# GpSimd's scatters of the second region wait, quad by quad, for TensorE's sums of the first

## The reference

```python
h = jnp.maximum(_layernorm(x, axis=-1), 0.0)
xw = feature @ weight
msgs = edge_weight[:, None] * xw[edge_col]            # one message of 128 floats per edge
agg = jax.ops.segment_sum(msgs, edge_row, num_segments=feature.shape[0])
new_feature = agg + bias                              # then batch norm, relu, two residuals
```

## Time and profile before

| | us |
|---|---|
| median of 3 runs | 5428.9 |
| lowest and highest | 5419.73, 5434.21 |
| span of the profiled execution | 5477.2 |
| TensorE busy (matmul) in it | 3042.5 |
| GpSimd busy in it | 3230.7 |

### The profile page before, as it was taken

One profiled execution on the slowest core, in us unless ns is written; L12 is line 12 of the kernel. 1 busy time (PEld: TensorE's weight loads), 2 busy tenths in 40 slices (PEclk: granted clock), 3 DMA queues, 4 the chain that ended last, 5 costly groups with the idle time before them and its releaser, 6 DMA issues.

```text
span 5477.2 us, 57778 instructions
## 1 busy us (share of the span) xinstructions
PE 3042.5 (56%) x16167; PEld 2620.6 (48%) x16167; DVE 2092.3 (38%) x5291; ACT 1457.9 (27%) x3880; POOL 3230.7 (59%) x3309
## 2 busy tenths in 40 slices
PE   6634444431595343333333787887785566666666
PEld 6534333321592232223223666766674455555555
DVE  8723222220362000000002444444445566666666
ACT  3211111100003232323333333333332233333332
POOL 2466666667203666666664666666663566666663
PEclk7666666665796555555555656555656777877778
DMA  3633333334463111111112333333332444444443
GB/s 103 185 106 114 115 112 111 108 128 130 160 232 118 45 45 47 44 47 45 47 45 71 94 90 93 90 94 93 91 94 77 121 133 133 133 134 132 132 134 85
DMA packets 262094, 563.24 MB, mean 103 GB/s; under 512 B 70904, under 2 KB 83065, under 8 KB 260860
## 3 DMA queue, kind: packets, MB, share of 16 engines
q0 software_dynamic: 119856, 280.99, 18.8%
q1 hardware_dynamic: 131858, 265.37, 14.6%
q10 hardware_dynamic: 10090, 13.23, 1.0%
HBM read 410.82 MB, written 150.10 MB: 102 GB/s over the span
## 4 chain that ended last, share of the span: by engine, by line
another core or an unknown queue 35%; PE 20%; issue 17%; DVE 15%; ACT 7%; DVEq 3%; POOL 1%; DMA 0%; ACTq 0%; POOLq 0%
ACT arena L897 4%; PE banks L1192 3%; PE banks L1179 3%; PE banks L1022 3%; PE banks L1002 2%; DVEq L1259 2%; PE banks L1009 2%; DVE work L1380 2%; ACT arena L904 2%; PE banks L1162 2%; PE banks L967 2%; DVE acc L1368 1%; DVE work L1867 1%; DVE work L1864 1%
## 5 line engine op out<-in xcount | busy, mean ns | idle before, releaser
L707 POOL DMA_INDIRECT work<-rel_table,idx_b x808 | 773.3, 957 | 682.9 <-DMA rel_table<-work 300.9
L723 POOL DMA_INDIRECT work<-kv_table,idx_a x808 | 776.3, 961 | 472.3 <-issue 217.1
L723 POOL DMA_INDIRECT work<-gat_table,idx_a x808 | 777.4, 962 | 469.9 <-issue 258.7
L692 POOL DMA_INDIRECT msgs<-work,idx_a x808 | 805.8, 997 | 394.4 <-issue 238.3
L1240 PE MATMUL banks<-work,arena 128*128 128x128 f32 x1616 | 387.4, 364 | 733.3 <-issue 661.2
L1022 PE MATMUL banks<-work,arena 128*128 128x136 f32 x3232 | 697.4, 375 | 66.6 <-issue 60.4
L790 ACT ACTIVATE arena<-iota,dst_local 128x128 f32<-128x128 f32 x1616 | 511.5, 388 | 733.8 <-remote 445.6
L1240 PEld LDWEIGHTS banks<-work,arena 128*128 128x128 f32 x1616 | 323.3, 266 | 800.8 <-issue 799.6
L1022 PEld LDWEIGHTS banks<-work,arena 128*128 128x128 f32 x3232 | 633.9, 277 | 102.6 <-issue 78.8
L1368 DVE TENSOR_TENSOR acc<-acc,banks 128x544 f32 x404 | 287.6, 712 | 921.2 <-remote 766.2
L1009 PE MATMUL banks<-nil 128*128 128x272 bf16 x1616 | 436.6, 363 | 36.6 <-issue 34.8
(11 more groups left out here) (320 smaller groups left out, 4701.2 us busy)
## 6 DMA issues: line engine op xcount, KB each, us to landing
work<-msgs SPq DMA_DIRECT2D x105, 516.0 KB
attr<-turned_all SPq DMA_DIRECT2D x204, 256.0 KB
turned_all<-work SPq DMA_DIRECT2D x202, 256.0 KB
w_rel<-turned_all SPq DMA_DIRECT2D x200, 256.0 KB
msgs<-work,idx_a POOLq DMA_INDIRECT x808
work<-rel_table,idx_b POOLq DMA_INDIRECT x808
work<-gat_table,idx_a POOLq DMA_INDIRECT x808
work<-kv_table,idx_a POOLq DMA_INDIRECT x808
```

What stands on the lines that cost most here:

```text
L692: nc.gpsimd.indirect_dma_start(msgs_all, bass.IndirectOffsetOnAxis(ap=idx_a[:, t:t + 1], axis=0), msg_ring[:, t % SPAN, :], None).then_inc ...
L707: nc.gpsimd.indirect_dma_start(row_ring[:, t % SPAN, :], None, rel_table, bass.IndirectOffsetOnAxis(ap=idx_b[:, t:t + 1], axis=0)).then_in ...
L723: nc.gpsimd.indirect_dma_start(ring[:, t % SPAN, :], None, table, bass.IndirectOffsetOnAxis(ap=idx_a[:, t:t + 1], axis=0)).then_inc(quad_i ...
```

## The change

Before each quad of region B, GpSimd now also waits until TensorE has summed a share of region A's halves. Quad `q` needs `82 * (q - 167) // 39` halves: none up to quad 167, then 2, 4, 6, 8, 10, 12, 14, 16, 18, 21 and so on, 71 for the last, quad 201. 34 quads have such a wait. Nothing is removed and no instruction changes its place on any engine.

```diff
+SUM_LAG = 4
...
+        def halves_due(q):
+
+            return HALVES_A * max(q - NQ_A - SUM_LAG, 0) // NQ_B
+
...
                 else:
                     late_wait(pool, q)
+                    if halves_due(q):
+                        pool.wait_ge(agg, at_agg["0b"] + HALF * halves_due(q))
                 for t in range(QUAD * q, QUAD * (q + 1)):
                     nc.gpsimd.indirect_dma_start(
```

## The result

| | before | changed |
|---|---|---|
| median of the timed runs, us | 5431.56 (4 runs, 5419.73 to 5440.97) | 5330.66 (4 runs, 5327.1 to 5334.71) |
| profiled execution, span, us | 5477.2 | 5332.9 |
| from the first scatter of region B to the last sum, us | 399.0 | 291.7 |
| of that, the scatters, us | 198.1 | 238.0 |
| from the last sum to the end, us | 3857.3 | 3824.2 |

What follows compares the result with a forecast made beforehand. Bound: scatters, then sums, in effect one after the other, as GpSimd's unbroken stream holds TensorE back. 11.3 cycles of 22.3 us, 252 us, then 61 us of sums: 60 us less, 5428.9 - 60 = 5369 us; range 5290 to 5560.

Steps and rivals of the forecast that it cites:

- holdback: Sums beside region B's scatters: TensorE's work held back and seen late, a half of 1.79 us taking 44.6.
- GpSimd's unbroken stream: Claimed cause: GpSimd's indirect DMAs without a break hold back what TensorE sends; a pause of GpSimd's lets it out.
- The first wait at 1246.5: Quad 168, which needs two halves, comes at 1246.5 us; GpSimd stops there.
- I take 7 us: Length of each GpSimd pause in region B, between 4.6 us (second layer) and 23.7 us (after the last scatter).
- After a pause the burst lasts 7 us: TensorE after each GpSimd pause: 3.9 halves in 7 us, as from 1231, plus some 2.6 done and not yet seen.
- GpSimd scatters three quads, 15.3 us: Scatters between two pauses in region B: 6.5 halves allow three quads, 15.3 us; with the pause, 22.3 us a cycle.
- the rival of nearly full overlap: First pause ends TensorE's delay, later stops keep it away: sums end at 1485, 134 us less, 5295 us; chance 0.12.
- After the scatters: Sums left once region B's scatters end: 34 halves, 61 us at full rate.
- A half beside GpSimd at 2.5 us: Sums beside scatters: loads, scatters and reloads share the DMA engines, so a half may take 2.5 us.
- Only SP waits for `msgs_done`: End of region B's scatters: only SP waits for `msgs_done`, at half 82, and its delay is covered.
- Long pauses: Rival: pauses of 23.7 us, a cycle 39 us, sums end at 1749.5: 130 us more, 5559 us; chance 0.26.
- the case in which only the profile changes: Rival: TensorE's delay comes from the recording, not the timed runs, which stay at 5429 us; chance 0.15.

Runs made afterwards that it cites:

- Serial order: Changed kernel with one wait, at quad 168, for all 71 halves of region A, and none after it: 5468.38 us, ratio 0.9988.
- landing waits: Kernel before, with GpSimd waiting at each quad from 168 on until the scatters of the quad before have landed: 5444.25 us, ratio 0.9941.
- spacer: Kernel before, with a GpSimd memset of 25,600 elements after each scatter from quad 168 on, no wait on the sums: 5371.51 us, ratio 0.9807.
- tiny spacer: Kernel before, with a GpSimd memset of one element per partition after each scatter from quad 168 on: 5446.51 us, ratio 0.9934.
- runs that change layer 2: Changed kernel with a memset of 25,600 elements after each row gather of layer 2 (5379.09 us, ratio 0.9818), or every second (5325.86 us, ratio 0.9813).
- one wait only: Changed kernel with only the first of its 34 waits kept (quad 168, two halves): 5452.88 us, ratio 0.9955.

## Why the prediction was right in kind and short in size

- **What bounds the stage: right.** The holdback was the loss. Serial order costs what before cost (ratio 0.9988), and two changes that never ask TensorE anything (landing waits, spacer) bring the overlap about.
- **It is GpSimd's unbroken stream: right, and shown** by three runs that change only that stream: the spacer run, the landing waits and, by halves, the tiny spacer. By what way the stream reaches TensorE is not shown.
- **The first wait at 1246.5: right.** 25.5 us after region B's first scatter were forecast; the pause began 25.8 us after it.
- **"I take 7 us" for a pause: too long.** Measured 4.2, 1.4, 4.9 and 1.5. The low end, from the 4.6 us of the second layer, was the right row; the 23.7 us after the last scatter were not. The 4.9 us of region A were misread: the 156.1 us hold one wait of 42.8 us, before the very first scatter; the other 31 average 3.7. In the two other profiles with the same region B (the runs that change layer 2) the first pause was 5.9 and 7.3 us, and all pauses together 14.7 and 10.7.
- **"After a pause the burst lasts 7 us": the step that failed.** It carried the burst from 1231 over to all others. The time without the full holdback was 111 us in the changed kernel (1247 to 1358, with one stop of 1.4 us in it), so there were two long pauses and two short ones, 12 us, where 11.3 cycles with 79 us of pauses were forecast. That is 67 us.
- **"GpSimd scatters three quads, 15.3 us": its rate was wrong the other way.** Without the pauses a quad took 5.9 us on average and not 5.1, 200 us for the 34 instead of 173. That is why the rival of nearly full overlap (134 us less) did not come either. The measured result lies between the two. From the first pause to the last scatter it took 212 us, 252 forecast: 67 us too many for pauses and 27 too few for quads. That the two errors have opposite signs brought the forecast nearer than its cycle deserves; so much of it is luck.
- **After the scatters: near.** 53.7 us of sums were left, 61 forecast.
- **A half beside GpSimd at 2.5 us: right on average, by luck.** 399 and 321 sums in 111 us are 45 halves, 2.5 us each. But the forecast took it from the shared DMA engines, and where they were 0.98 and 0.99 busy a half took 1.9 and 2.0 us; the slow stretch, 4.3 us a half, had them at 0.72.
- **"Only SP waits for `msgs_done`": incomplete.** VectorE waits for it too, after its last one-hot matrix; this costs nothing in the sum.
- **Long pauses: did not come.** None in the changed kernel's trace was over 5 us.
- **The recording: not settled.** The profiled span fell with the medians, which refutes the case in which only the profile changes. But the slowest timed run, 5334.71 us, is the profiled span plus 1.8, and each of the other three also has a span 1.8 us below its time and a granted clock on record, so nothing here shows that any of them ran without a recorder. The Trainium skill ("NOTIFIC — the notification-queue block", section 7.1, Overflow) says that the block always pushes back inside itself rather than lose a record, and that stalls counted there would mean a throttled engine; it gives no time per record. A price per instruction that does not depend on its size, 2.8 us for a matmul with its load, fits that rule. It would also be expected of any other thing sent once per instruction. No run tells these apart, and no run here shows what the change is worth without a recorder.

**Still open.** What lengthens the scatters beside a running TensorE. VectorE by itself is excluded. In the changed kernel the DMA engines are 0.78 busy over 1231 to 1420, against 0.38 before, and landing waits beside loads took 4 to 6 us against 2.1 without, so the loads' traffic is my guess; no run had loads without sums. Open too is why a burst ends: one wait alone held TensorE free for 20 us, the 34 waits for 111. And open is why a pause of 4 us is enough at one place and 23 us are needed at another. After the last scatter TensorE was at its full rate again only 23 us later in the kernel before and 17 us later with one wait only, both after a long dense stream, but within 1 and 3 us with the tiny spacer and with the memset after every second scatter. That would fit a backlog that a dense stream builds up and that has to drain; no run tests it.

## What to carry to other kernels

When an engine shows single instructions at a constant distance, idle for "issue", and its results are seen long after they are done, look for another engine with an unbroken stream of small DMAs, and measure by putting 0.15 us between them before anything is reordered. Bear in mind that such a loss may come with the recording: no run here could tell. Waits that rarely hold are a cheap net: they cost 12 us here and ended the one full relapse (after 37 us, since a wait holds only once TensorE is behind its share), where a wait at every quad on something always late cost 112. A spacer pays only where what it frees is the bound: in region B it brought 105 us, in layer 2 it cost what it saved. And a coincidence of two engines in a timeline is not a cause; the one event that releases both may be it.

## What the runs showed of the hardware that was not expected

- The holdback charges per instruction: 2.80 us for a matmul with its load, f32 128x128 or bf16 128x8 alike, in steps of 0.7 us.
- 0.15 us in each gap of GpSimd's stream (1.266 to 1.413 us) keeps it away, some 20 us after the spacing began; in every second gap it about halves it and does nothing for the time.
- While TensorE is held back, GpSimd stops too: in the run with the tiny spacer 34 times, 19.4 us, before a 0.11-us memset whose only wait is for its own memset before.
- With seven tiny bf16 matmuls among sixteen f32 ones TensorE did not get its full clock. Both kernels come out of the holdback, with its single matmuls, at 0.50. By stretch, the kernel before and the one with more instructions, both with GpSimd still and TensorE always busy:

```profile
1460.00:1600.00 140.00, 140.00 (x1256) 140.00 (x1256) 109.03 (x157) 0.00 (x0) 0.00 (x0) 1.00 0.88 297
```

```profile
1460.00:1800.00 340.00, 340.00 (x1595) 309.73 (x1595) 96.05 (x138) 0.00 (x0) 0.00 (x0) 0.50 0.37 108
```

  The granted clock was 0.50, the lower of the two levels, through all 340 us, instead of 1.00, and a half took 4.9 us instead of 1.79. With the 100 halves summed after the scatters, this is most of the 322 us that this kernel lost. It was measured once, and the share of the clock in the 4.9 us is not separated from that of the seven instructions.
- VectorE at 10 us on end beside GpSimd's indirect DMAs changed neither's duration (0.96 and 1.25 us).
